# Attention and experts layer on one core: a block's weighted sums issued behind the next block's shift

## The chip, the cores and the metric

The kernel runs on one core of a Trainium2 chip. The metric is device time in microseconds (us) of the whole kernel, the median of several executions. Lower is better.

## The reference

The input is 16 batches of 512 tokens by 128 features, float32. Each batch goes through layernorm, an attention step and an expert step, each added back to its input:

```
qkv = layernorm(x) @ qkv_w.T                  # 16 heads of 8 features
c = mean of q per block . mean of k per block # 8 blocks of 64 tokens
mask: a block of queries sees its own block of keys and its one best block
x = x + softmax(q k / sqrt(8), masked) @ v @ proj_w.T + proj_b
logits = layernorm(x) @ wr + br               # 4 experts, the best 2 are kept
y_e = gelu(layernorm(x) @ w1_e + b1_e) @ w2_e + b2_e
x = x + sum over the kept experts of gate_e * (y_e, corrected by a constant)
```

## The kernel before, in words

Every engine has its own program, written out in order by hand (functions `tensor`, `vector`, `scalar`, `pool`, `sync`); the engines meet only at semaphores. TensorE, VectorE and ScalarE each run a loop over the batches b (0 to 15) and in it over the 8 blocks m of 64 queries. The work is software-pipelined over batches: while batch b has its attention, the second products of the experts of batch b - 2 are computed (`c_down`), the projections q, k, v of batch b + 1 (`project`), and behind the blocks the first products of the experts of batch b - 1 (`c_up`). Full overlap begins at b = 2.

TensorE's steps for one block m, b at least 2, in the order of lines 469 to 506:

- `weighted(b, m-1)` (L349, 32 matmuls): values times probabilities of the block before, into o_ps. It waits for the exponentials and for the copy of the values.
- `row_max(b, m)` (L329, two transposes): turns the maxima over the keys, which VectorE found (`block_max`, L657), into v_ps. It waits until v_ps is free.
- `scores(b, m+1)` (L310, 4 matmuls), into the other half of s_ps.
- `shift(b, m)` (L338, 16 matmuls): subtracts the row maxima from the scores in PSUM. It waits for VectorE's `row_max` (L666), which makes nmax from what TensorE's `row_max` turned.
- `o_rows` (L356, four transposes, blocks 2, 4, 6): a pair of blocks of weighted sums is turned back, after ScalarE has copied it (`o_copy`, L932). `o_columns` (L363, blocks 3, 5, 7) and `o_project` (L368, blocks 4, 6) follow for the pair.
- In blocks 2, 3, 4 `project` q, k, v of the next batch (L264 to L266); in block 5 the products of the block means (L293), from which VectorE selects the best key block (`a_select`, L637 to L648, ending in the index for a gather by DMA on POOL, L1030). In block 1 `a_columns` (L273) turns the next batch's normalised rows.
- `c_down` chunks 2m and 2m+1 (L406, two matmuls each). Four chunks make one expert's output in the bank y_ps, so a bank is complete with the last chunk of blocks 1, 3, 5 and 7.
- `values(b, m+1)` (L322): turns the next block's values into v_ps; ScalarE copies them to vaug (L917), which frees v_ps.

After block 7 follow `weighted(b, 7)`, the projection of pair 2 and 16 `c_up` steps; behind the 13th of them `begin(b + 1)` issues the next batch's first scores, which wait for the gathered keys (DMA keys<-kv_chosen).

VectorE's order in a block (L808 to L853): `row_max(b, m)` (L666), `block_max(b, m+1)` (L657), `o_project`, `o_rows` (reciprocal L673, product L676), then work of the other batches: in block 1 `a_columns` (L597), in block 2 sums and parts of q (L601, L606, L607), in block 3 the low part of k and the product of sums (L612, L613, L630), in block 5 the selection, in block 6 the ranking and split (L711 to L723, L702); last in odd blocks `c_gated(b - 2, m // 2)` (L753), which reads the completed bank y_ps.

ScalarE's order in a block (L970 to L989): in blocks 2, 4, 6 `o_copy` (L932), then `shift_exp` (L924, the exponentials), then copies of the projections (L897, L910, L905), `o_columns` (L939) and `values` (L917).

The lines that tie VectorE's two steps to TensorE's:

```
pe.wait_ge(bank_v.free, bank_v.at["max", b, m])       # L334, shift waits for VectorE's row_max
v.wait_ge(bank_v.full, bank_v.at["max", b, m])        # L663, VectorE's row_max waits for TensorE's
v.wait_ge(of.full, of.at["down", b, e])               # L745, c_gated waits for the fourth chunk
act.wait_ge(weighted_done, 2 * n + 2)                 # L929, o_copy waits for both blocks' sums
```

Of the kernel before, what the change touches and what calls it, by code (L numbers as in the profile page):

```python
# [21 lines left out]
M = N // BS  # L22
# [41 lines left out]
def layer(nc, x, wqkv_t, wproj_t, proj_b, w1, b1_t, w2, b2, wr, br, ident, head_sum,  # L64
          head_one, block_rank, row_mine, row_base, expert_before, expert_rows, own_block, head_mask,
          query_rows, key_rows, out):
    with ExitStack() as ctx:
# [172 lines left out]
        def stages(b):  # L240


            return (2, 0, 1, 3) if b == 0 else (2, 3, 4, 5)
# [18 lines left out]
        def tensor(pe):  # L262
# [13 lines left out]
            def a_columns(b):  # L276
                pe.wait_ge(xn_done, b + 1)
                columns(b, "xnT", xn)
# [188 lines left out]
            for b in range(B):  # L467
                ahead = b >= 1 and b + 1 < B
                for m in range(M):
                    if m >= 1 and b >= 2:  # L470
                        weighted(b, m - 1)
                    row_max(b, m)
                    if m >= 1 and b < 2:
                        weighted(b, m - 1)
                    edge = m in (0, M - 1)
                    if b >= 2 and edge:
                        c_down(b - 2, 2 * m)
                    if m + 1 < M:
                        scores(b, m + 1)
                    shift(b, m)  # L480
                    if b == 0 and m >= 3 or b == 1 and m not in (2, 3, 4):
                        keep_busy(5)
                    if b >= 1 and m == 0:
                        c_columns(b - 1)
                    if b >= 1 and m == 1:
                        c_route(b - 1, (2, 3))
                    if m in (2, 4, 6):
                        o_rows(b, (m - 2) // 2)
                    if m in (3, 5, 7):
                        o_columns(b, (m - 3) // 2)  # L490
                    if m in (4, 6):
                        o_project(b, (m - 4) // 2)
                    if ahead and m in stages(b)[:3]:
                        project(b + 1, "qkv"[stages(b).index(m)])
                    if ahead and m == stages(b)[3]:
                        a_products(b + 1)
                    if b >= 2 and not edge:
                        c_down(b - 2, 2 * m)
                    if ahead and m == 1:
                        a_columns(b + 1)  # L500
                    if b >= 2:
                        c_down(b - 2, 2 * m + 1)
                    if m + 1 < M:
                        values(b, m + 1)
                    if b >= 1 and m == 0:
                        c_route(b - 1, (0, 1))
                    if b == 0:
                        if m in stages(b)[:3]:
                            project(b + 1, "qkv"[stages(b).index(m)])
                        if m == stages(b)[3]:  # L510
                            a_products(b + 1)
                        if m >= 5:
                            (bias_out, bias_sum, bias_columns)[m - 5]()
# [17 lines left out]
            b = B - 1  # L531
# [31 lines left out]
        def vector(v):  # L563
# [242 lines left out]
            for b in range(B):  # L806
                ahead = b >= 1 and b + 1 < B
                for m in range(M):  # L808
# [19 lines left out]
                        block_max(b, m + 1)  # L828
                    if m in (4, 6):
                        o_project(b, (m - 4) // 2)  # L830
                    if m in (2, 4, 6):
                        o_rows(b, (m - 2) // 2)
                    if ahead and m == 0:
                        a_rows(b + 1)
# [14 lines left out]
                        c_gates(b - 1, ranked)  # L849
                    if b >= 2 and m % 2:  # L850
                        c_gated(b - 2, m // 2)
                    if b == 0 and m == 2:
                        bias_masked()  # L853
                o_project(b, T - 2)
# [16 lines left out]
            b = B - 1  # L871
# [20 lines left out]
        def scalar(act):  # L892
# [75 lines left out]
            values(0, 0)  # L968
            for b in range(B):
                for m in range(M):  # L970
                    if m in (2, 4, 6):
                        o_copy(b, (m - 2) // 2)
                    shift_exp(b, m)
                    if b >= 1 and m == 0:
                        c_columns(b - 1)
                    if b >= 1 and b + 1 < B and m == 1:
# [590 lines left out]
```

## Time and profile before

| | |
|---|---|
| median of 3 executions | 893.54 us (892.5 to 895.87) |
| the profiled execution: its time, its span | 900.17 us, 898.5 us |
| TensorE matmul busy, weight loads busy | 827.9 us (92%), 558.8 us (62%) |
| VectorE busy, ScalarE busy | 517.5 us (58%), 460.9 us (51%) |
| TensorE's granted clock, mean | 0.962 of full speed |

Busy times are sums of instruction durations. Matmuls are pipelined and their ends are modelled, so the distance from one group's start to the next group's start says more of TensorE's pace than its busy share. In the rows, PE is TensorE's matmul queue, PEld its weight loads, DVE VectorE, ACT ScalarE, POOL GpSimd. Idle time in square brackets is what the engine sat idle just before the group, and who released it.

### The profile page before, as it was taken

What the parts mean: (1) busy time and instruction counts of PE and PEld (TensorE: products, weight loads), DVE (VectorE), ACT (ScalarE), POOL (GpSimd) and SP (SyncE); (2) the same over time, 40 slices, a digit from 0 to 9 for tenths busy, and PEclk for the clock granted to TensorE, in tenths of its full rate; (3) what the DMA queues carried; (4) which work ended last, traced back from release to release, by engine and by line L of the source; (5) the groups of instructions that cost most, each with busy time, mean ns of one, the idle gap of its engine ahead of it and who ended that gap; (6) DMA issues with size and microseconds to landing.
All of it is one profiled execution on the core that took longest, in us unless ns stands there. A gap on an engine that the chain in (4) does not pass through costs nothing.

```text
span 898.5 us, 23529 instructions
## 1 busy us (share of the span) xinstructions
PE 827.9 (92%) x9382; PEld 558.8 (62%) x9382; DVE 517.5 (58%) x1526; ACT 460.9 (51%) x754; POOL 174.8 (19%) x176
## 2 busy tenths in 40 slices
PE   3287889999999999999999999999999999999995
PEld 2165667666666666676666567676666666666662
DVE  6073465746575665747566565757566666646321
ACT  2042247374655556374746457374646556473740
POOL 5300011210313031221213021221213031211111
PEclk8598599999999999999999999999999999999998
DMA  8987078676958668685957578675848676771110
GB/s 257 231 213 172 5 215 182 165 178 185 214 155 210 167 184 195 187 193 164 212 159 193 151 199 194 191 191 158 213 145 215 164 204 160 210 159 35 60 59 13
DMA packets 207440, 151.77 MB, mean 169 GB/s; under 512 B 123208, under 2 KB 189648, under 8 KB 203232
## 3 DMA queue, kind: packets, MB, share of 16 engines
q1 hardware_dynamic: 205024, 133.46, 59.8%
q0 software_dynamic: 2304, 16.78, 5.0%
q8 instruction: 76, 1.25, 0.6%
q14 instruction: 36, 0.29, 0.1%
HBM read 95.02 MB, written 50.99 MB: 163 GB/s over the span
## 4 chain that ended last, share of the span: by engine, by line
PE 61%; DMA 20%; ACT 8%; issue 5%; DVE 3%; SPq 2%; POOL 0%; POOLq 0%; ACTq 0%; DVEq 0%
PE y_ps L406 15%; DMA selected<-kv_table,index 8%; PE o_ps L349 6%; PE s_ps L310 5%; DMA kv_chosen<-selected 4%; PE s_ps L338 4%; PE s_ps L264 4%; ACT hid L960 4%; PE s_ps L266 4%; PE s_ps L265 4%; DMA kv_table<-stage 3%; PE o_ps L356 3%; PE a_ps L379 2%; PE v_ps L329 2%; DMA keys<-kv_chosen 2%
## 5 line engine op out<-in xcount | busy, mean ns | idle before, releaser
L406 PE MATMUL y_ps<-hid,w2s 128*128 128x512 f32 x480 | 236.1, 602 | 0.0
L657 DVE TRANSPOSE_TENSOR_REDUCE rmax<-s_ps 128x16 bf16<-128x512 f32 x256 | 168.2, 699 | 70.5 <-PE s_ps L310 70.4
L924 ACT ACTIVATE prob<-s_ps 128x1024 f32<-128x1024 f32 x128 | 131.1, 1024 | 150.6 <-PE s_ps L338 150.5
L960 ACT ACTIVATE hid<-s_ps,b1s 128x512 f32<-128x512 f32 x256 | 171.2, 688 | 38.8 <-PE s_ps L266 35.2
L1050 POOL TENSOR_TENSOR yT<-yT,gate_cols 128x512 f32<-128x512 f32 x48 | 61.4, 1279 | 294.7 <-DVE gate_cols L753 294.2
L310 PE MATMUL s_ps<-qdiag,keys 128*128 128x256 f32 x512 | 95.3, 309 | 24.8 <-DMA keys<-kv_chosen 24.7
L264 PE MATMUL s_ps<-xnhi,w1hi 128*128 128x512 f32 x256 | 113.1, 442 | 1.4
L406 PEld LDWEIGHTS y_ps<-hid,w2s 128*128 128x128 f32 x480 | 83.2, 193 | 43.8 <-issue 40.0
L917 ACT COPY vaug<-v_ps 128x128 f32<-128x128 f32 x128 | 33.9, 265 | 147.4 <-PE v_ps L322 147.3
L666 DVE TENSOR_REDUCE nmax<-v_ps 128x64 bf16<-128x256 bf16 x128 | 54.2, 423 | 95.4 <-PE v_ps L329 95.4
L266 PE MATMUL s_ps<-xnhi,w1lo 128*128 128x512 f32 x256 | 101.4, 396 | 0.0
L265 PE MATMUL s_ps<-xnlo,w1hi 128*128 128x512 f32 x256 | 100.9, 394 | 0.0
L349 PEld LDWEIGHTS o_ps<-prob,vaug 128*32 128x32 f32 x4096 | 64.1, 111 | 54.9 <-issue 41.8
L310 PEld LDWEIGHTS s_ps<-qdiag,keys 128*128 128x128 f32 x512 | 71.0, 195 | 39.0 <-issue 30.3
L349 PE MATMUL o_ps<-prob,vaug 128*32 128x64 f32 x4096 | 85.0, 224 | 0.0
L338 PEld LDWEIGHTS s_ps<-nmax,hone 64*128 64x128 bf16 x2048 | 37.7, 96 | 36.6 <-DVE nmax L666 32.7
L264 PEld LDWEIGHTS s_ps<-xnhi,w1hi 128*128 128x128 f32 x256 | 48.4, 189 | 19.1 <-ACT hid L960 8.8
L338 PE MATMUL s_ps<-nmax,hone 64*128 64x64 bf16 x2048 | 53.0, 193 | 4.9 <-DVE nmax L666 3.7
L266 PEld LDWEIGHTS s_ps<-xnhi,w1lo 128*128 128x128 f32 x256 | 48.1, 188 | 11.6
L932 ACT COPY oT<-o_ps 128x512 f32<-128x512 f32 x64 | 37.5, 587 | 32.5 <-PE o_ps L349 32.5
L265 PEld LDWEIGHTS s_ps<-xnlo,w1hi 128*128 128x128 f32 x256 | 48.7, 190 | 6.4 <-issue 0.7
L1030 POOL DMA_INDIRECT selected<-kv_table,index x16 | 17.7, 1104 | 157.6 <-DVE index L648 151.0
(143 smaller groups left out, 1051.5 us busy)
## 6 DMA issues: line engine op xcount, KB each, us to landing
qdiag<-q_table SPq DMA_DIRECT2D x128, 128.0 KB, 3.9
kv_chosen<-selected SPq DMA_DIRECT2D x32, 512.0 KB, 5.5
keys<-kv_chosen SPq DMA_DIRECT2D x32, 512.0 KB, 5.4
gate_cols<-gates SPq DMA_DIRECT2D x64, 256.0 KB, 4.2
kv_table<-stage SPq DMA_DIRECT2D x16, 768.0 KB, 3.9
q_table<-qpair SPq DMA_DIRECT2D x16, 512.0 KB, 3.0
xs<-in_x SPq DMA_DIRECT2D x16, 256.0 KB, 5.7
kv_table<-stage SPq DMA_DIRECT2D x16, 256.0 KB, 2.9
```

What stands on the lines that cost most here:

```text
L264: pe.matmul(dst, left_hi, right_hi, start=True, stop=False)
L265: pe.matmul(dst, left_hi, right_lo, start=False, stop=False)
L266: return pe.matmul(dst, left_lo, right_hi, start=False, stop=True)
L310: ins = pe.matmul(s_ps[i][:, g * HQ * BS:(g + 1) * HQ * BS].rearrange("p (h s) -> p h s", s=BS), keys[j][:, m, g, :], queries, start=g % 2 ...
L338: ins = pe.matmul(s_ps[i][:, half * N + h * BS:half * N + (h + 1) * BS], hone[r, h, :], nmax[i][r, :], start=False, stop=True, skip_group_ ...
L349: ins = pe.matmul(o_ps[32 * (h % HQ):32 * (h % HQ) + VW, h // HQ, i * BS:(i + 1) * BS], vaug[i][:, h, :], prob[i][:, h, :], start=True, st ...
L406: ins = pe.matmul(dst[:], w2s[:, n, :], hid[:, n, :], start=(c == 0), stop=(c == C - 1))
L657: v.tensor_reduce(rmax[m % 2][:, :, half * P // 2:half * P // 2 + HH].rearrange("p k h -> p h k"), s_ps[m % 2][:, half * N:(half + 1) * N] ...
L666: v.tensor_reduce(nmax[m % 2][:].rearrange("h (b c) -> h b c", b=2), v_ps[:, 0:P].bitcast(BF16).rearrange("h (b g c) -> h b c g", b=2, g=4 ...
L924: act.activation(prob[m % 2][:].rearrange("p h s -> p (h s)"), s_ps[m % 2][:], ACT.Exp, scale=SCALE).then_inc(exped, 1)
L960: act.activation(hid[:, k, :], up_ps[up_bank(k)], ACT.Gelu, bias=b1s[:, k:k + 1]).then_inc(gelued, 1)
L1050: g.tensor_tensor(yT[:], yT[:], gate_cols[(E * b + e) % NG][:], ALU.add).then_inc(summed, 1)
```

## The change

For b of at least 2, TensorE issues `weighted(b, m-1)` behind `shift(b, m)` instead of ahead of `row_max(b, m)`. `values(b, m+1)` and, in blocks 2, 4, 6, `o_rows` now stand ahead of the last chunk of `c_down` (2m+1); `o_rows` stood right behind `shift` before. VectorE takes its `o_rows` at the end of the block, behind `c_gated`, and ScalarE its `o_copy` behind `shift_exp`. For b = 0 and 1 all stays in place but that `values` moves in the text past lines that do nothing there. No instruction is added or removed.

```diff
@@ tensor
                 for m in range(M):
-                    if m >= 1 and b >= 2:
-                        weighted(b, m - 1)
                     row_max(b, m)
                     if m >= 1 and b < 2:
                         weighted(b, m - 1)
...
                     shift(b, m)
+                    if m >= 1 and b >= 2:
+                        weighted(b, m - 1)
...
-                    if m in (2, 4, 6):
+                    if m in (2, 4, 6) and b < 2:
                         o_rows(b, (m - 2) // 2)
...
                     if ahead and m == 1:
                         a_columns(b + 1)
+                    if m + 1 < M:
+                        values(b, m + 1)
+                    if m in (2, 4, 6) and b >= 2:
+                        o_rows(b, (m - 2) // 2)
                     if b >= 2:
                         c_down(b - 2, 2 * m + 1)
-                    if m + 1 < M:
-                        values(b, m + 1)
@@ vector
-                    if m in (2, 4, 6):
+                    if m in (2, 4, 6) and b < 2:
                         o_rows(b, (m - 2) // 2)
...
                     if b >= 2 and m % 2:
                         c_gated(b - 2, m // 2)
+                    if m in (2, 4, 6) and b >= 2:
+                        o_rows(b, (m - 2) // 2)
@@ scalar
-                    if m in (2, 4, 6):
+                    if m in (2, 4, 6) and b < 2:
                         o_copy(b, (m - 2) // 2)
                     shift_exp(b, m)
+                    if m in (2, 4, 6) and b >= 2:
+                        o_copy(b, (m - 2) // 2)
```

## Rows read from the trace of the kernel before

**Rows 1.** The page, part 1: busy time and share of the span by engine.

```profile
PE 827.9 (92%) x9382; PEld 558.8 (62%) x9382; DVE 517.5 (58%) x1526; ACT 460.9 (51%) x754; POOL 174.8 (19%) x176
```

**Rows 2.** The timeline of PE, two batches' same step (start us, us, engine, line, operation).

```profile
440.80 0.60 PE L422 MATMUL y_ps<-idn,yT 128*128 128x128 f32 x4
...
490.30 0.60 PE L422 MATMUL y_ps<-idn,yT 128*128 128x128 f32 x4
```

**Rows 3.** The timeline of PE and PEld at the head of block 3.

```profile
411.50 0.65 PE L349 MATMUL o_ps<-prob,vaug 128*32 128x64 f32 x32
...
412.08 0.28 PE L329 MATMUL v_ps<-idn,rmax 128*128 128x128 bf16 x2
412.15 0.54 PEld L310 LDWEIGHTS s_ps<-qdiag,keys 128*128 128x128 f32 x4
...
412.89 0.29 PEld L338 LDWEIGHTS s_ps<-nmax,hone 64*128 64x128 bf16 x16 [0.20 <-DVE nmax L666]
...
413.23 0.33 PE L363 MATMUL v_ps<-idn,att 128*128 128x128 f32 x1
```

**Rows 4.** The waits by engine: us in total, times, longest us.

```profile
PEld s_ps L338 <- DVE nmax L666: 32.7, 101, 3.1
...
PE s_ps L310 <- DMA keys<-kv_chosen: 24.7, 6, 16.9
...
PEld o_ps L349 <- ACT prob L924: 11.6, 14, 0.8
```

**Rows 5.** The timeline of PE and DVE, end of block 1 and head of block 2.

```profile
405.50 1.02 PE L406 MATMUL y_ps<-hid,w2s 128*128 128x512 f32 x2
...
406.32 0.69 DVE L597 TENSOR_TENSOR xnlo<-a_ps,xnhi 128x512 fp32r<-128x512 f32 x1 [0.61 <-ACT xnhi L897]
406.36 0.27 PE L322 MATMUL v_ps<-idn,vals 128*128 128x128 f32 x1
...
406.93 0.74 DVE L753 SCALAR_TENSOR_TENSOR yT<-y_ps,mT,gate_cols 128x512 f32<-128x512 f32 x1
407.15 0.29 PE L329 MATMUL v_ps<-idn,rmax 128*128 128x128 bf16 x2
...
407.59 0.41 DVE L666 TENSOR_REDUCE nmax<-v_ps 128x64 bf16<-128x256 bf16 x1
...
408.06 0.41 PE L338 MATMUL s_ps<-nmax,hone 64*128 64x64 bf16 x16
```

**Rows 6.** The timeline of ACT and DVE, end of block 3 and head of block 4.

```profile
414.29 0.58 ACT L910 CAST stage<-a_ps 128x512 fp32r<-128x512 f32 x1
...
416.11 0.22 DVE L630 TENSOR_TENSOR qk<-qsum,ksum 128x64 f32<-128x64 f32 x1
...
416.25 0.75 DVE L753 SCALAR_TENSOR_TENSOR gate_cols<-y_ps,mT,gate_cols 128x512 f32<-128x512 f32 x1
...
416.92 0.42 DVE L666 TENSOR_REDUCE nmax<-v_ps 128x64 bf16<-128x256 bf16 x1
```

**Rows 7.** The timeline of PE and DVE, end of block 5 and head of block 6.

```profile
423.14 1.94 PE L406 MATMUL y_ps<-hid,w2s 128*128 128x512 f32 x4
...
425.12 0.75 DVE L753 SCALAR_TENSOR_TENSOR gate_cols<-y_ps,mT,gate_cols 128x512 f32<-128x512 f32 x1
...
426.03 0.42 DVE L666 TENSOR_REDUCE nmax<-v_ps 128x64 bf16<-128x256 bf16 x1 [0.16 <-PE v_ps L329]
```

**Rows 8.** The timeline of PE and PEld, end of block 7.

```profile
431.71 1.02 PE L406 MATMUL y_ps<-hid,w2s 128*128 128x512 f32 x2
...
432.73 0.49 PEld L349 LDWEIGHTS o_ps<-prob,vaug 128*32 128x32 f32 x32 [0.83 <-ACT prob L924]
```

**Rows 9.** The timeline of PE: the longest wait for gathered keys after the start.

```profile
496.77 0.71 PE L310 MATMUL s_ps<-qdiag,keys 128*128 128x256 f32 x4 [2.03 <-DMA keys<-kv_chosen]
```

**Rows 10.** Windows: us, busy of PE, PEld, DVE, ACT, POOL, granted clock, DMA.

```profile
345.80:348.00 2.20, 2.10 (x11) 1.64 (x11) 1.32 (x2) 0.63 (x2) 0.00 (x0) 1.00 1.12 252
...
499.50:502.00 2.50, 2.50 (x8) 1.36 (x8) 0.42 (x1) 1.97 (x2) 0.00 (x0) 0.55 0.70 146
```

**Rows 11.** The timeline of PE: the wait for keys ahead of the first window above.

```profile
345.84 0.71 PE L310 MATMUL s_ps<-qdiag,keys 128*128 128x256 f32 x4 [1.30 <-DMA keys<-kv_chosen]
```

## The prediction, made before the changed kernel was run

> **What bounds the kernel now.** I read the page first, then the timeline of one steady batch, then the waits. By the page TensorE is busy nearly throughout and no other engine is busy for more than 58% of the span [rows 1]. The timeline says what a batch costs: the same step of two neighbouring batches starts 49.5 us apart [rows 2]. Within that stretch the matmul groups follow each other almost without a gap, so the batch is the sum of TensorE's steps, which run in program order, and of the short waits between them. A reordering that adds and removes nothing can therefore change only the waits.
>
> Which waits are there? Block 3 is typical [rows 3]. weighted takes 0.58 us from start to start (411.50 to 412.08). row_max starts at 412.08, the weights of the scores are loaded from 412.15 to 412.69, and shift's first weights only at 412.89: 0.20 us of waiting for nmax. From row_max to shift it is thus 0.81 us, and shift takes 0.34 us to the next step (413.23). This wait returns in nearly every block: 32.7 us of weight-load idling in 101 cases, some of it under running matmuls [rows 4]. What makes it is the round trip row_max on TensorE, nmax on VectorE, shift on TensorE. VectorE's nmax starts 0.32 to 0.33 us behind row_max's start when VectorE is free (412.08 to 412.41 in block 3, of which the row in block 6 shows the same: it follows row_max with 0.16 us of idling before it [rows 7]), takes 0.42 us, and shift starts 0.06 us after its end.
>
> The second thing to see is how nearly VectorE is late. In block 2 it comes from the low part of the normalised rows (406.32 to 407.01), goes at once into c_gated (406.93) and from that at once into nmax (407.59), which is 0.44 us behind row_max instead of 0.33 [rows 5]. Shift starts at 408.06, 0.91 us behind row_max. In block 4 c_gated (416.25 to 417.00) runs into nmax (416.92) with nothing between, on top of the chain of k: high part on ScalarE, sums and low part on VectorE, qk [rows 6]. In block 6 only 0.16 us is spare [rows 7]. In other words the time that VectorE needs for c_gated behind the last chunk of an odd block is hidden today by two of TensorE's steps: values and weighted, together 0.79 us (406.36 to 407.15 [rows 5]), 0.21 and 0.58.
>
> **The change, part by part.**
>
> *weighted behind shift, values ahead of the last chunk.* This takes both covers away. TensorE now goes from the last chunk straight to row_max, while c_gated cannot start before the last chunk has ended. And nothing is put between row_max and shift, so the 0.20 us stay. I follow the batch of the rows.
>
> Block 1: the weighted sums of block 0 move behind its shift, everything after them keeps its time; a_columns of the next batch and the chunk behind it too.
>
> Block 2: values takes the place at 405.50, the last chunk starts at 405.71 and row_max at 406.57 (a chunk takes 0.86 us, 405.50 to 406.36 [rows 5]), 0.58 us earlier than before. VectorE is no earlier: the low part still ends at 407.01; the bank is complete at 405.71 + 1.02 = 406.73, so c_gated starts at 406.93, nmax at 407.59, shift at 408.06, all as before. But weighted is then still to be done: **+0.58 us**.
>
> Block 3: VectorE's o_rows, some 0.5 us in two operations, now comes last in block 2, behind the parts of q. By my reckoning it ends about when nmax of block 3 is wanted. Bounds: 0 (it fits) and 0.10. I take **+0.04 us**.
>
> Block 4: the projection of k stands behind weighted, so it is 0.62 us later, and the whole chain of rows 6 with it, since it has no slack: shift comes 0.62 us later than before, with weighted of block 3 still to do: another **+0.58 us**.
>
> Block 5: block 4 is even, it has no c_gated; o_rows (two operations, about 0.5 us) ends before row_max's result is there. 0.
>
> Block 6: if the last chunk of block 5 starts at X, it ends at X + 1.02, c_gated starts at X + 1.06 (it started 0.04 us behind the end of the chunks, 425.08, in rows 7), nmax 0.67 us later as in rows 5 and 6 at X + 1.73, and shift at X + 1.73 + 0.42 + 0.06 = X + 2.21. Unhindered it would be X + 0.86 + 0.81 = X + 1.67. **+0.54 us**.
>
> Block 7: a chunk stands between row_max and shift and hides VectorE's ranking, split and o_rows; 0. Behind it weighted(b, 7) waited for its exponentials: it started at 432.73, the chunk before it at 431.71, a chunk is 0.86, so 0.16 us were lost [rows 8], in 14 batches [rows 4]. With weighted(b, 6) now in between this goes: **-0.16 us**.
>
> *exponentials ahead of the pair's copy; o_rows late.* ScalarE's exponentials come up to 0.6 us earlier in blocks 2, 4, 6, but nobody waits for them there. The copy starts about 1.0 us behind shift and o_rows is asked for some 2.4 us behind it, under weighted, projection and chunk; that cover is enough, so 0. Without it the copy (0.6 us) would show. The copy of values (0.27 us) must be done before row_max; its cover is the last chunk, 0.86 us, so 0. The result goes on to o_columns a block later, unaffected. On SP and POOL nothing is moved.
>
> *The gathered keys.* Four times after the start the next batch's first scores wait for keys, 1.0 to 2.0 us (24.7 us in 6 cases with 16.9 at the start [rows 4]; the longest is in rows 9). The gather hangs on the selection in block 5, which is delayed by 0.58 + 0.04 + 0.58 = 1.20 us, while the scores are delayed by 1.58; these waits shrink by 0.38 us each: **-1.5 us** over the kernel.
>
> **Sum.** 0.58 + 0.04 + 0.58 + 0.54 - 0.16 = 1.58 us a batch by the rows; I take 1.5, as small successions (transposes before a chunk rather than before other short steps) may give back some hundredths. The order changes for b = 2 to 15, 14 batches: +21.0, less 1.5: +19.5 us. The profiled execution had 900.17 us (span 898.5), so 919.7 there. That is 6.63 us above the median of 893.54, much of it the waits for keys; against the median it makes **913.0 us**.
>
> **Rivals.**
>
> 1. *VectorE is late only in block 2* (the others have some slack that starts do not show): 14 x (0.58 - 0.16) = +5.9, 899.4 us; with one more block 907. For it: only block 2 shows a late nmax already. Against: rows 6 and 7 have 0 and 0.16 us of slack, and 0.79 us of cover go. Chance 0.08.
>
> 2. *The clock falls as well.* After a wait of 2.03 us for keys [rows 9] the granted clock of a stretch of 2.5 us was 0.55, about the lower of its levels, 1.2 GHz [rows 10]; that cost 2.5 x 0.45 = 1.1 us. After a wait of 1.30 us [rows 11] it was full, 2.4 GHz [rows 10]. The new waits are about 0.7 us, three times a batch. If they brought such a fall once a batch, that adds 14 x 1.1 = 15.4: 928 us. [...] Chance 0.04.
>
> 3. *No change.* VectorE gets c_gated done in time after all (the bank is complete earlier than the modelled ends say), and only the 0.16 us are gained: 14 x 0.16 = 2.2, 891.3 us. Chance 0.08.
>
> 4. *Faster.* The wait of shift for nmax vanishes, because row_max starts earlier in the block. By rows 3 it is 0.20 us of loading; in 7 blocks of 14 batches 98 x 0.20 = 19.6, plus 2.2: 872 us. It decides where nmax ends before the scores' weights are in, 0.61 us behind row_max's start; nmax's own round trip is 0.33 + 0.42 + 0.06 = 0.81. That speaks against it, as nothing enters between the two. The Trainium skill (Trainium Kernel Development and Optimization, "Best Practices") would have the distance to the limit judged by the weight loads' busy share, not the matmuls'; by that, 62% leaves room for such a gain, but the timeline shows TensorE's matmul groups following each other without gaps, whatever the share of the loads. Chance 0.04.
>
> **How the numbers follow.** The forecast has 0.76. A measurement of this kernel can tell about 0.5% (4.5 us) from no change. Slower by more than that: forecast, rivals 1 and 2, 0.88; same 0.08; faster 0.04. The range reaches from rival 1 with a second block late (some way below 907) to the forecast with all terms at their upper ends (1.7 a batch, nothing given back at the keys: 917) and a few falls of the clock: 903 to 922.
>
> **What would show it.** Batches 51 us apart in the steady part instead of 49.5. In blocks 2, 4, 6 the weight load of shift idles 0.7 to 0.9 us for nmax, in 3, 5 still 0.2; c_gated starts right behind the last chunk or the low part, and nmax right behind c_gated, 1.0 us behind row_max instead of 0.33. weighted(b, 7) no longer waits for exponentials. The waits for keys are a little shorter. I am wrong if nmax in block 2 starts earlier than 0.9 us behind row_max, or if the copy of values or o_rows shows up as what TensorE waits for.

## The result, and the profile after

The changed kernel takes **903.12 us** (median of 7 executions, 900.37 to 904.16). The kernel before takes 892.5 us on the same chip (7 executions, 890.39 to 899.19). The ratio is 1.0106, 95% interval 1.0078 to 1.0133: 10.6 us slower, where 19.5 had been forecast. The profiled execution after has 900.37 us and a span of 898.7 us, which is 0.2 us more than the span before; why that is not the change's cost is worked out below.

The page, part 1, of the kernel after:

```profile
PE 811.9 (90%) x9382; PEld 550.7 (61%) x9382; DVE 520.3 (58%) x1526; ACT 455.9 (51%) x754; POOL 175.1 (19%) x176
```

TensorE is busy for less time than before (827.9 us in [rows 1]) in an equal span: the time is in waits. The waits by engine after (us in total, times, longest us):

```profile
PEld s_ps L338 <- DVE nmax L668: 56.6, 101, 3.6
...
PE s_ps L338 <- DVE nmax L668: 28.4, 45, 3.4
...
PE s_ps L310 <- DMA keys<-kv_chosen: 17.7, 2, 17.3
PEld v_ps L322 <- ACT attT L943: 17.4, 32, 1.3
...
PEld o_ps L349 <- ACT prob L928: 10.8, 15, 0.8
```

Beside [rows 4] this says two things. Shift's wait for VectorE has grown from 32.7 to 56.6 us, and now the matmuls wait as well as the weight loads, 45 times (28.4 us; before, 3 times and 3.7 us). The scores' wait for the gathered keys has gone from 24.7 us in 6 cases to 17.7 in 2, of which 17.3 are the start. One change made TensorE wait more and less.

The head of block 2 after, in the timeline of all engines, answers to [rows 5]:

```profile
400.00 1.02 PE L406 MATMUL y_ps<-hid,w2s 128*128 128x512 f32 x2
...
400.71 0.69 DVE L599 TENSOR_TENSOR xnlo<-a_ps,xnhi 128x512 fp32r<-128x512 f32 x1 [0.62 <-ACT xnhi L901]
...
400.99 0.27 PE L329 MATMUL v_ps<-idn,rmax 128*128 128x128 bf16 x2
...
401.32 0.74 DVE L755 SCALAR_TENSOR_TENSOR yT<-y_ps,mT,gate_cols 128x512 f32<-128x512 f32 x1
401.98 0.41 DVE L668 TENSOR_REDUCE nmax<-v_ps 128x64 bf16<-128x256 bf16 x1
...
402.44 0.41 PE L338 MATMUL s_ps<-nmax,hone 64*128 64x64 bf16 x16 [0.65 <-DVE nmax L668]
...
402.78 0.65 PE L349 MATMUL o_ps<-prob,vaug 128*32 128x64 f32 x32
```

row_max starts at 400.99. VectorE is still at the low part (to 401.40), takes c_gated, and reaches nmax 0.99 us behind row_max, where it took 0.44 before; shift's matmuls wait 0.65 us. Weighted comes behind them and covers nothing. The starts of shift in the eight blocks of this batch, from TensorE's timeline after:

```profile
393.72 0.41 PE L338 MATMUL s_ps<-nmax,hone 64*128 64x64 bf16 x16
...
397.12 0.41 PE L338 MATMUL s_ps<-nmax,hone 64*128 64x64 bf16 x16
...
402.44 0.41 PE L338 MATMUL s_ps<-nmax,hone 64*128 64x64 bf16 x16 [0.65 <-DVE nmax L668]
...
407.26 0.41 PE L338 MATMUL s_ps<-nmax,hone 64*128 64x64 bf16 x16
...
412.42 0.41 PE L338 MATMUL s_ps<-nmax,hone 64*128 64x64 bf16 x16 [0.54 <-DVE nmax L668]
...
417.43 0.41 PE L338 MATMUL s_ps<-nmax,hone 64*128 64x64 bf16 x16
...
421.91 0.41 PE L338 MATMUL s_ps<-nmax,hone 64*128 64x64 bf16 x16 [0.54 <-DVE nmax L668]
...
426.54 0.41 PE L338 MATMUL s_ps<-nmax,hone 64*128 64x64 bf16 x16
```

From shift to shift both kernels do the same work (one weighted lies between them in either order; only in the first stretch there is none after, so 0.58 us are added to its 3.40, and the last stretch, to weighted(b, 7), has one too many, so 0.58 is taken off):

| stretch | before, us | after, us | difference |
|---|---|---|---|
| block 0 to 1 | 4.07 | 3.98 | -0.09 |
| 1 to 2 | 4.74 | 5.32 | +0.58 |
| 2 to 3 | 4.83 | 4.82 | -0.01 |
| 3 to 4 | 4.51 | 5.16 | +0.65 |
| 4 to 5 | 5.07 | 5.01 | -0.06 |
| 5 to 6 | 4.04 | 4.48 | +0.44 |
| 6 to 7 | 4.70 | 4.63 | -0.07 |
| 7 to weighted(b, 7) | 1.52 | 1.46 | -0.06 |

The sum is +1.38 us. The steady batch has gone from 49.5 us [rows 2] to 50.87 (the step of [rows 2] starts at 385.79 and 436.66), that is +1.37.

**Where the time went.** The same step lies in every batch, the first time at the end of b = 2. Its first start fell at 189.46 us before and 182.15 after; over the profiled executions of all kernels here this start varied between 182 and 194 us, and the code up to b = 1 is the same, so these 7.3 us are not put down to the change. The clock has a part in them: in the first 190 us the mean granted clock was 0.85 of full speed before and 0.91 after. The twelve batches that follow took 603.59 us before and 610.97 after. Before, 12 x 49.5 make 594.0, and the other 9.6 lie in every third batch (51.61, 51.2, 53.4 and 51.26 us long), those that wait for keys. Not all of the 9.6 is waiting for keys: the four waits of the first scores are 5.9 us (1.51, 1.30, 2.03 and 1.03), some more is waiting for the gathered values just behind them, and in the batch of 53.4 us about 1.5 us is the clock. After the wait of 2.03 us it fell to its lower level. The windows of before and of after have

```profile
498.00:502.00 4.00, 4.00 (x13) 2.27 (x12) 1.03 (x3) 2.78 (x4) 0.00 (x0) 0.57 0.86 184
```

```profile
190.00:840.00 650.00, 623.96 (x7487) 420.15 (x7486) 403.44 (x1174) 358.74 (x598) 124.27 (x122) 1.00 0.67 173
```

where the third number from the end is the granted clock: about half before in those 4 us, in which the batch's lag behind its neighbours grew from 2.4 us (at 497.52) to 3.9 (at 504.29), and full after in all twelve batches.

After, 12 x 50.87 make 610.4, and 0.5 is left. So the twelve batches lost 12 x 1.37 = 16.4 us in the order of the steps and got back 9.1 at the keys: +7.4 net. With b = 2 as well that is about 8.8, and the executions say 10.6, between 7.0 and 11.9 by the interval. In b = 15 next to nothing was lost (47.61 against 47.72 us).

**Why the waits for keys are gone.** Each batch writes its keys to a table in DRAM (768 KB), the values behind it, and then, once the write has landed, reads its own keys from it (SP's queue). The page, part 3, has a queue of instruction packets (packets, MB, share of the same 16 DMA engines):

```profile
q8 instruction: 76, 1.25, 0.6%
```

They are 16 KB each. I take them to be the fetches of TensorE's program: nothing names them so, but filler matmuls, which change TensorE's program alone, move them (see e13 and e14). The timeline of SP before, in a batch whose successor's scores waited 2.03 us [rows 9]:

```profile
469.52 0.38 SPq L1111 DMA_DIRECT2D kv_table<-stage  x1
469.94 2.26 SPq L1115 DMA_DIRECT2D vals<-stage  x1
...
474.54 0.73 SPq L1121 DMA_DIRECT2D keys<-kv_table  x1
```

and the DMA queues before in the stretch 469 to 470 us (packets, MB, share of 16 engines):

```profile
q8 instruction: 1, 0.02, 6.4%
```

One instruction packet, 6.4% of sixteen engines over 1 us, so one engine for about 1 us. It starts some 0.5 us behind the write's issue, and the keys are read 5.0 us behind it. After the change, in the batch that answers to it:

```profile
466.09 0.38 SPq L1117 DMA_DIRECT2D kv_table<-stage  x1
466.52 0.67 SPq L1121 DMA_DIRECT2D vals<-stage  x1
470.06 0.73 SPq L1127 DMA_DIRECT2D keys<-kv_table  x1
```

Here the keys are read 3.97 us behind. Over the whole kernel before, a packet fell 0.5 to 0.8 us behind the write in exactly every third batch (writes at 168.67, 319.29, 469.52, 621.92 and 772.26 us); there the keys were read 4.6 to 5.2 us behind the write, in all others 4.0. In the profile after, packets fall at about -2.5, -1.0 and +4.9 us from the write, and it is 4.0 to 4.1 always.

From the late write to TensorE's wait the way is long. Behind the four writes that a wait followed, the gather's instruction on POOL starts up to 0.4 us later than elsewhere, the gathered rows land 15.5 to 16.6 us behind the write (14.2 to 14.7 in the steady batches between), and the first of the gathered keys 26.0 to 27.0 us behind it (23.2 to 23.8). The first scores ask for them 25.2 us behind it. Why the delay of about 1 us has grown to some 3 by then is not shown. All this is so far two traces side by side; the second half of the experiments is about it.

### The profile page after: what moved, and what is told of

It reads as the page before. It is cut to its first block, busy times and chain, and to the rows that moved or that the text cites. A ratio compares the mean times of both kernels' runs of the same rounds, so it can differ in the third digit from the quotient of the medians.

```text
span 898.7 us, 23529 instructions
## 1 busy us (share of the span) xinstructions
PE 811.9 (90%) x9382; PEld 550.7 (61%) x9382; DVE 520.3 (58%) x1526; ACT 455.9 (51%) x754; POOL 175.1 (19%) x176
## 4 chain that ended last, share of the span: by engine, by line
PE 69%; DMA 10%; ACT 8%; issue 6%; DVE 4%; SPq 2%; POOL 0%; DVEq 0%; POOLq 0%; ACTq 0%
PE y_ps L406 19%; PE o_ps L349 7%; PE s_ps L264 5%; PE s_ps L338 5%; PE s_ps L266 4%; PE s_ps L265 4%; ACT hid L964 4%; DMA selected<-kv_table,index 4%; PE s_ps L310 4%; PE o_ps L356 3%; DMA kv_chosen<-selected 3%; PE v_ps L368 2%; PE a_ps L379 2%; DVE nmax L668 2%; ACT L928 2%
## 5 line engine op out<-in xcount | busy, mean ns | idle before, releaser
L406 PE MATMUL y_ps<-hid,w2s 128*128 128x512 f32 x480 | 245.5, 600 | 0.0
L310 PE MATMUL s_ps<-qdiag,keys 128*128 128x256 f32 x512 | 93.2, 305 | 17.7 <-DMA keys<-kv_chosen 17.7
L406 PEld LDWEIGHTS y_ps<-hid,w2s 128*128 128x128 f32 x480 | 78.3, 194 | 14.2 <-issue 10.0
L338 PE MATMUL s_ps<-nmax,hone 64*128 64x64 bf16 x2048 | 52.6, 192 | 28.7 <-DVE nmax L668 28.4
L338 PEld LDWEIGHTS s_ps<-nmax,hone 64*128 64x128 bf16 x2048 | 37.3, 95 | 60.3 <-DVE nmax L668 56.6
L349 PEld LDWEIGHTS o_ps<-prob,vaug 128*32 128x32 f32 x4096 | 63.1, 110 | 17.3 <-ACT prob L928 10.8
L329 PEld LDWEIGHTS v_ps<-idn,rmax 128*128 128x128 bf16 x256 | 22.1, 102 | 63.7 <-issue 58.1
```

The source lines that it names most:

```text
L310: ins = pe.matmul(s_ps[i][:, g * HQ * BS:(g + 1) * HQ * BS].rearrange("p (h s) -> p h s", s=BS), keys[j][:, m, g, :], queries, start=g % 2 ...
L338: ins = pe.matmul(s_ps[i][:, half * N + h * BS:half * N + (h + 1) * BS], hone[r, h, :], nmax[i][r, :], start=False, stop=True, skip_group_ ...
L349: ins = pe.matmul(o_ps[32 * (h % HQ):32 * (h % HQ) + VW, h // HQ, i * BS:(i + 1) * BS], vaug[i][:, h, :], prob[i][:, h, :], start=True, st ...
L406: ins = pe.matmul(dst[:], w2s[:, n, :], hid[:, n, :], start=(c == 0), stop=(c == C - 1))
```

## The experiments

Three questions: is the loss VectorE's c_gated in front of nmax; is the gain the fetches beside the table write; and, what came up on the way, why some executions of the kernel before are longer than others. The expectations name some theories by letter; the fetch in the table write stands against the new order by itself (later scores, other neighbours on the queues) as what took the waits away. Runs that stand together in a paragraph with one number for the kernel before ran on the same chip.

### Is it VectorE's order?

**e4**: the kernel after, and on VectorE `c_gated` behind the next block's `row_max`. TensorE keeps the new order.

```diff
                     row_max(b, m)
+                    if b >= 2 and m in (2, 4, 6):
+                        c_gated(b - 2, m // 2 - 1)
...
-                    if b >= 2 and m % 2:
+                    if b >= 2 and m == M - 1:
                         c_gated(b - 2, m // 2)
```

> The changed kernel, with VectorE's c_gated of blocks 1, 3 and 5 taken behind row_max of the next block (2, 4, 6) instead of ahead of it. Theory A (VectorE comes late to nmax because c_gated starts only behind the last chunk, which row_max now follows at once): nmax starts 0.33 us behind row_max in blocks 2, 4 and 6, the batch falls from 50.87 to 49.3 us and the time to 880 to 884 us. Rival (the lateness comes from the copies or from o_rows that moved): blocks 2, 4 and 6 keep 0.5 us or more of waiting and the time stays within 4 us of 903.

Measured: 884.57 us against 900.1 of the kernel before, ratio 0.9822 [0.9748, 0.9895]; batches of 49.33 us. The timeline of all engines in e4, head of block 2:

```profile
449.55 0.69 DVE L599 TENSOR_TENSOR xnlo<-a_ps,xnhi 128x512 fp32r<-128x512 f32 x1 [0.62 <-ACT xnhi L903]
...
449.83 0.27 PE L329 MATMUL v_ps<-idn,rmax 128*128 128x128 bf16 x2
...
450.16 0.42 DVE L668 TENSOR_REDUCE nmax<-v_ps 128x64 bf16<-128x256 bf16 x1
450.49 0.74 DVE L755 SCALAR_TENSOR_TENSOR yT<-y_ps,mT,gate_cols 128x512 f32<-128x512 f32 x1
450.63 0.29 PEld L338 LDWEIGHTS s_ps<-nmax,hone 64*128 64x128 bf16 x16 [0.20 <-DVE nmax L668]
```

nmax is back at 0.33 us behind row_max and c_gated follows it. e4's waits show what is left of shift's:

```profile
PEld s_ps L338 <- DVE nmax L668: 31.9, 101, 3.1
```

56.6 us have become 31.9, the value of before [rows 4]. Everything else of the change is in e4, so the whole loss per steady batch (50.87 - 49.33 = 1.54 us) is c_gated in front of nmax, and the rest of the change gives 49.5 [rows 2] - 49.33 = 0.17 us a batch. Some of e4's batches are longer (up to 50.42 us), in part because `values` waits for the gathered values.

**e10**: the kernel after, with `values` behind the last chunk again, so that row_max's wait for v_ps stands without cover.

```diff
-                    if m + 1 < M:
-                        values(b, m + 1)
                     if m in (2, 4, 6) and b >= 2:
                         o_rows(b, (m - 2) // 2)
                     if b >= 2:
                         c_down(b - 2, 2 * m + 1)
+                    if m + 1 < M:
+                        values(b, m + 1)
```

> The changed kernel, but with values(b, m+1) behind the last chunk again, so that row_max follows values at once. Theory A (row_max must wait for ScalarE's copy of values, 0.31 + 0.27 + 0.06 = 0.64 us behind its start, where weighted hid it before): row_max comes 0.43 us later behind values than their 0.21 us in blocks 3 to 7; in blocks 4 and 6 this takes the place of most of the wait for c_gated. Batches of 51.5 to 52.5 us, 912 to 926 us. Rival (only c_gated delays, the copy is hidden): 50.7 to 50.9 us as in the changed kernel, 905 us.

Measured: 933.46 us in one execution (before: 894.85); batches of 52.63 us. Both are somewhat above what was expected, 912 to 926 and 51.5 to 52.5. The waits of e10:

```profile
PE v_ps L329 <- ACT vaug L921: 42.1, 93, 0.8
```

row_max now waits for ScalarE's copy of the values, 0.45 us each time in steady blocks, where after the change this wait is 4.2 us in 8 cases, all told. Once weighted no longer stands between values and row_max, values has to go ahead of a chunk: the two moves of the change belong together.

### Is shift's 0.20 us for nmax a loss? (rival 4)

**e6**: e4 with weighted between row_max and scores, so that shift is asked for 0.58 us later and nmax is ready.

```diff
-                    if m >= 1 and b < 2:
+                    if m >= 1:
                         weighted(b, m - 1)
...
                     shift(b, m)
-                    if m >= 1 and b >= 2:
-                        weighted(b, m - 1)
```

> The changed kernel with c_gated of blocks 1, 3, 5 behind the next row_max and with weighted(b, m-1) between row_max and scores instead of behind shift. Theory A (the 0.2 us that shift waits for nmax are a round trip which weighted covers, once neither c_gated nor the copy of values delays row_max): from row_max to shift 1.22 us with the weighted sums in it, instead of 0.80 plus 0.58; 0.16 us less in each of blocks 1 to 6, batches of 48.4 us instead of 49.33, 870 to 874 us. Rival (the keys become the bound, since the gather is asked for earlier by less than the scores): waits for keys of 0.5 to 1 us in most batches, 880 us.

Measured: 908.46 us against 901.09, ratio 1.0091 [1.0061, 1.0121]; batches of 51.02 us. That is at least 34 us more than expected. TensorE's timeline in e6:

```profile
477.50 0.27 PE L329 MATMUL v_ps<-idn,rmax 128*128 128x128 bf16 x2
477.71 0.65 PE L349 MATMUL o_ps<-prob,vaug 128*32 128x64 f32 x32
478.29 0.73 PE L310 MATMUL s_ps<-qdiag,keys 128*128 128x256 f32 x4
478.96 0.41 PE L338 MATMUL s_ps<-nmax,hone 64*128 64x64 bf16 x16
```

From scores to shift it is 0.67 us although nmax has long been there, against 0.71 in [rows 3] (412.18 to 412.89). The "0.20 <- nmax" before shift's weight load was nearly all hidden under the scores' own matmuls: 0.04 us of it was loss. And row_max to weighted takes 0.21 us rather than 0.10 to the scores, so that row_max to shift with weighted in it takes 1.46 us in the plain blocks, more than the 0.79 + 0.58 of the kernel after. Weighted right behind row_max also waits for what is made late: in block 3 row_max to shift took 1.84 us, in block 7 mostly 2.07. Rival 4's 19.6 us were not there to be had.

### Are the waits for keys the fetches in the table write?

The idea: if the fetches come at fixed places of TensorE's program, adding or removing filler matmuls at the start (`keep_busy`, two instructions per unit) moves them against the writes. Only that number is edited:

```diff
-            keep_busy(16)
+            keep_busy(20)
```

20 in e2, 40 in e7, 48 in e13, 52 in e14 for the kernel before; 12 in e3 and 34 in e8 for the kernel after.

**e1, e2, e3** (before: 900.1 us). The kernel before once more, and both with a little filler more or less:

> The kernel before once more, for a second profile of it. Theory A (the cause is in the program): TensorE's batches are again 49.5 us apart but for every third one, which is 1.7 to 3.9 us longer because the first scores of the next batch wait for the gathered keys, and in just these batches the 16 KB instruction packet on queue q8 starts 0.5 to 0.8 us behind the issue of the table write (kv_table<-stage, 768 KB), so that the keys of the own block are issued 4.6 to 5.2 us behind it instead of 4.0. Theory B (chance of the profiled execution): the waits stand in other batches or are gone, and the time is nearer to 885 us.

> The kernel before with 4 more idle matmuls (8 instructions with their weight loads) in TensorE's warm-up at the start, where it waits for data anyway; all code after it lies 8 instructions further on. Theory A (the keys come late where an instruction fetch of TensorE falls into the table write): the fetch in every third batch moves from +0.6 us to about -1.0 us relative to the write's issue, the write takes 4.0 us everywhere, the waits for keys go, 882 to 886 us. Theory B (the waits come from the period of the transfers or from chance): nothing changes, 892 us with waits of 1 to 2 us in every third batch.

> The changed kernel with 4 fewer idle matmuls in the warm-up. Theory A: the fetches that stand 1.0 us ahead of the table write in every third batch move to about +0.6 us, the write takes 4.6 to 5.2 us there, and the waits for keys come back in every third batch, smaller than before (0.5 to 1.5 us): 905 to 909 us against 903 of the changed kernel. Theory B (the later scores of the changed order hide the keys whatever the fetches do): 903 us, no waits.

e1: 901.82 us; fetches 0.5 to 1.7 us behind the write in every third batch and own keys read 4.9 to 5.5 us behind it, much as in the first trace, so the pattern belongs to the program. Once more it came in a batch that is not a third one (write at 723.57 us): there the fetch was at +0.6 and the keys at 5.15, where the first trace has the fetch at -0.5 and 3.95 in the same batch. e2: 900.04 us, ratio 0.9993 [0.9956, 1.003], fetches at +0.6 to +1.0, late writes as before (4.4 to 5.2). e3: 905.16 us, ratio 1.0051 [1.0012, 1.0091], fetches at about -2, -0.1 to -1.2 and +4.9, all writes 4.0 to 4.1, no waits for keys in the steady batches. Eight instructions hardly move a fetch, so e2 and e3 decide nothing. e3 has batches of 50.87 us as the kernel after. But e1 had batches of 50.35 us, not 49.5; on that see below.

**e7, e8** (before: 901.09 us).

> The kernel before with 24 more idle matmuls (48 instructions) in the warm-up. The 8 instructions of the first try hardly moved the fetches. Theory A (fetches in the table write make it late): the fetch of every third batch leaves the range 0 to 3.5 us behind the write's issue for about -1 us, and the own keys are issued 4.0 us behind the write in all batches; if another batch's fetch enters the range instead, that batch has the late write. Theory B (what is late is that batch, not the fetch): the write stays late by 0.6 to 1.2 us in the same batches 2, 5, 8, 11, 14 wherever the fetch stands.

> The changed kernel with 18 more idle matmuls (36 instructions) in the warm-up. Theory A: in every third batch a fetch enters the range 0 to 3.5 us behind the table write's issue, the own keys are issued 4.5 to 5.2 us behind it there instead of 4.0, and a wait for keys of up to 1 us shows. Theory B: the write takes 4.0 us everywhere as in the changed kernel, whose batches are 50.87 us.

e7: 902.94 us; the fetch of the third batches stayed at +0.5 to +1.3 and their keys at 5.1 to 5.2 behind the write. Other fetches moved to +5.4, without effect. No decision. e8: 909.88 us; the fetch at +4.9 moved to +3.8 to +4.0, the end of the write. The timeline of SP in e8:

```profile
470.32 0.38 SPq L1117 DMA_DIRECT2D kv_table<-stage  x1
470.75 0.66 SPq L1121 DMA_DIRECT2D vals<-stage  x1
476.25 0.73 SPq L1127 DMA_DIRECT2D keys<-kv_table  x1
```

5.93 us instead of 3.97. In the five batches with such a fetch it was 4.58, 4.45, 5.93, 5.94 and 4.54, in all others 3.96 to 4.06. Behind the two of 5.9 waits for what is gathered were back in the new order of steps, 0.84 us for values and 1.21 us for keys, in batches of 52.79 and 52.43 us. So the order by itself doesn't take them away: the fetch theory holds, the other falls. (e8 is one execution, and its 909.88 us are not compared.)

**e13, e14** (before: 892.74 us), the test from the other side: the kernel before, with the fetches moved out.

> The kernel before with 32 more idle matmuls (64 instructions) in the warm-up. In e2 and e7 (8 and 48 instructions) the fetch of every third batch stayed 0.6 us behind the table write's issue. Theory A (the fetch makes the write late, the late write the waits for keys): with 64 instructions it leaves the write, the own keys are issued 4.0 us behind the write in those batches, the waits for keys go, and the median is 5 to 9 us below the kernel before on the same chip (less where block 6 waits for nmax and hides them). Theory B (it is the batch, not the fetch): the write stays late by 0.6 to 1.2 us in batches 2, 5, 8, 11, 14, ratio 1.0.

> The same with 36 more idle matmuls (72 instructions), in case 64 are not enough. Theory A: as for 64 instructions; whichever batches have a fetch between 0 and 4 us behind the write's issue, these and only these have the own keys issued later than 4.1 us behind it. Theory B: as there.

e13: 892.14 us, ratio 0.9976 [0.9942, 1.001]. The packet came at +0.4 to +0.5 in four of the five third batches (keys read 5.0 to 5.2 us behind the write) and at -0.6 in one, at 315.70 us; there it was 3.96, and its batch 49.5 us. e14: 890.8 us, ratio 0.9967 [0.9943, 0.9992], the packets at -0.5 to -0.9 in all five. The timeline of SP in e14:

```profile
461.93 0.38 SPq L1111 DMA_DIRECT2D kv_table<-stage  x1
462.35 0.67 SPq L1115 DMA_DIRECT2D vals<-stage  x1
...
465.89 0.73 SPq L1121 DMA_DIRECT2D keys<-kv_table  x1
```

its DMA queues from 461 to 462 us, and its waits:

```profile
q8 instruction: 1, 0.02, 7.0%
```

```profile
PE s_ps L310 <- DMA keys<-kv_chosen: 11.8, 3, 9.1
```

The packet is there, but ahead of the write. 3.96 us; all but one of the writes have 3.96 to 4.04 (one 4.38, with a fetch at +3.6). Eleven of the twelve batches are 49.5 to 49.6 us. The other, the first, has 50.56: it waits 0.65 us for gathered values and has the late write of 4.38. Of the three waits for keys that are left none lies in the twelve. So the kernel before has lost them in its old order, by 36 more units of filler (72 instructions) at its start. The profiled execution has a span of 886.1 us.

Over all 16 traces there are 224 such writes from b = 2 on. Behind the 36 with a fetch 0.4 to 1.7 us after their issue the own keys were read 4.40 to 5.68 us after it, behind the 9 with one at 3.6 to 4.0 us 4.05 to 5.94, behind the 9 at 4.2 to 4.4 us 4.02 to 4.42, and behind the other 170 3.95 to 4.13, with one exception of 4.33. No fetch fell between 1.7 and 3.6 us. This settles for the profiled executions what made the writes late and the waits come.

The medians don't confirm the size. e14 is 0.3% faster, 1.9 us, where 5 to 9 had been expected, and e13 0.2%, not told from nothing. The filler itself costs nothing that the trace shows: it ends at 32.8 us, and the first scores wait for keys until 41.91 (42.18 before). Nor is it the clock: straight lines through time against mean granted clock put e14's executions only 1.6 us below those of the kernel before at 0.972. The other executions were not profiled, so why they gain so little stays open. The median of the kernel after speaks for a gain at the keys of about 7 us: 13 x 1.37 = 17.8 were lost by the order and 10.6 measured.

### What else: block 6 in some sessions

In e1 the kernel before had 0.85 us more in block 6 of nine of the twelve batches. All engines of e1 there:

```profile
477.02 1.10 POOL L1030 DMA_INDIRECT selected<-kv_table,index  x1 [7.25 <-DVE index L648]
...
477.12 0.29 PE L329 MATMUL v_ps<-idn,rmax 128*128 128x128 bf16 x2
...
478.40 0.59 ACT L932 COPY oT<-o_ps 128x512 f32<-128x512 f32 x1 [1.49 <-PE o_ps L349]
478.44 0.42 DVE L666 TENSOR_REDUCE nmax<-v_ps 128x64 bf16<-128x256 bf16 x1 [1.15 <-PE v_ps L329]
...
478.92 0.41 PE L338 MATMUL s_ps<-nmax,hone 64*128 64x64 bf16 x16 [0.99 <-DVE nmax L666]
```

c_gated had long ended (477.29); row_max's result was there; yet VectorE's nmax and ScalarE's copy both start only at 478.4, some 0.3 us behind the end of POOL's gather instruction. In the first session, and in those of e9 to e12 and e13 and e14, nmax starts 0.32 us behind row_max in this block; in the sessions of e1 to e4 and e5 to e8 it was 1.17 to 1.36 in most batches of the old order. That fits with the 900.1 and 901.09 us that the kernel before has there and the 892.5 to 894.85 in the others (nine times 0.85 make 7.7 us). It is not a matter of the chip alone: e5 to e8 and e13 and e14 ran on the same one.

In these sessions it goes with the place of POOL's instruction. Of the 36 batches of e1, e2 and e7 it starts 0.09 to 0.26 us ahead of row_max in 26, and there nmax is 1.17 to 1.36 us behind row_max; in the other 10, where a late table write had pushed it to 0.07 to 0.47 us behind row_max, nmax is 0.32 to 0.74 us behind.

**e5**: the kernel after in such a session.

> The changed kernel, timed beside the kernel before on the chip of the coming runs. In the last runs the kernel before took 900 us on its chip instead of 892.5, its batches 50.35 us instead of 49.5, because in block 6 nmax started 1.17 us behind row_max instead of 0.32, where POOL's gather instruction stood. Theory A (the changed order keeps row_max of block 6 out of the gather instruction's way): 903 to 906 us here too, batches of 50.87 us, so that the loss against the kernel before is 1.1% on one chip and about 0.4% on another. Theory B (the chip slows both alike): 911 us, ratio 1.011.

905.06 us against 901.09, ratio 1.0043 [1.0011, 1.0074]; batches of 50.87 us, without the hold-up: in the new order the gather instruction starts 0.24 us *behind* row_max's start. So the change costs 1.1% in one kind of session and 0.4 to 0.5% in the other (e5 and e3), with the same 903 to 905 us of its own.

**e9, e11, e12** (before: 894.85 us). e9 is the kernel before with e4's edit on VectorE, e11 is e4 once more, and e12 lets POOL's gather wait for the matmuls of row_max in block 6:

```diff
+                if b >= 3:
+                    g.wait_ge(bank_v.full, bank_v.at["max", b - 1, 6])
```

> The kernel before, with c_gated of blocks 1, 3, 5 behind the next row_max as in e4, and nothing else. Theory A (in the old order values and weighted hide c_gated, so its place hardly matters): block 2 gains the 0.10 us that nmax was late there, batches 0.1 us shorter than those of the kernel before on the same chip, ratio 0.997 to 1.0. Rival (the gain of e4 is that of c_gated's place alone, whatever TensorE's order): about 885 us.

> The kernel of e4 once more, for a second interval. If its gain is real: batches of 49.3 to 49.6 us and 882 to 887 us, ratio 0.975 to 0.99. If it was the luck of one set of executions: within 5 us of the kernel before.

> The kernel before, with POOL's gather instruction waiting besides for TensorE's row_max of block 6, so that it starts about 0.3 us behind row_max's start instead of 0.27 us ahead of it. Theory A (where nmax of block 6 is 1.2 us behind row_max on this chip, the gather instruction, which starts between weighted and row_max, holds up what VectorE and ScalarE wait for): nmax follows row_max by 0.33 us again, batches of 49.5 us where the keys are there in time; the gather is 0.6 us later, so more batches wait for keys; 893 to 899 us. Theory B (the lateness has nothing to do with the gather's moment): nmax stays 1.2 us behind, batches 50.4 us and longer, 901 us or more.

e9: 894.91 us, ratio 0.9997 [0.996, 1.0033]; batches of 49.4 us, 0.1 shorter, but the keys waits stayed (27.6 us in 7 cases in its waits, every third batch): the edit on VectorE alone is worth nothing. e11: 883.17 us, ratio 0.9882 [0.982, 0.9944], steady batches of 49.12 us, five of the twelve longer (49.4 to 50.6): the version of both orders together beats both kernels in this kind of session too. e12: 895.88 us, ratio 1.0 [0.9966, 1.0034]. This chip had no hold-up to remove (batches of 49.5 us in either), so e12 tells nothing of it; it shows only that the gather, issued 1.34 us later, took 7.3 to 9.4 us rather than the 8.8 to 10.9 of the first trace, and the keys were hardly later. Whether POOL's instruction itself holds the two engines or something that goes with it, and why in two sessions only, stays open.

## Why the prediction was half right

- **The bound and the method**: right. TensorE is in order and gapless, and the change touched waits alone.
- **Block 2, +0.58**: measured +0.58 from shift to shift; nmax 0.99 us behind row_max, forecast 1.0.
- **Block 3, +0.04**: measured -0.01; nmax at 0.36 us instead of 0.33, so o_rows did just fit.
- **Block 4, +0.58**: +0.65. Of this 0.54 is nmax. The rest is, as I read it, an item that the prediction put at nothing ("The result goes on to o_columns a block later, unaffected"): o_columns now comes while values is asked for earlier, and values waits for ScalarE's copy of attT (17.4 us of weight-load idling in 32 cases; from the chunk's start at 409.04 to values at 410.05 it takes 1.01 us rather than the 0.86 of a chunk, 0.15 lost).
- **Block 6, +0.54**: nmax came exactly that late (shift 1.34 us behind row_max instead of 0.80), the stretch grew by 0.44.
- **Block 7, -0.16**: only -0.06. The exponentials are no longer late (they end at 428.01, weighted starts at 428.58), although the row still names them; but TensorE takes 0.95 us from the chunk to weighted all the same. A wait's name had long been done.
- **"Small successions may give back some hundredths"**: they gave back 0.06 to 0.09 in blocks 1, 5 and 7 each. Per batch +1.37 against 1.5 taken: a size, over 13 batches 1.7 us. And b = 15, counted as the 14th with 1.5 us, lost 0.11.
- **The 0.20 us of [rows 3]**: read as a loss in nearly every block. By e6 it was 0.04, the rest being hidden; the forecast kept it on both sides, so only rival 4 hung on it.
- **The gathered keys, -1.5 us**: this is the step that failed. "These waits shrink by 0.38 us each" took them as a transfer of fixed length against which the scores come a little later. Measured is -9.1 us in the twelve steady batches: the transfer's own length came from a 16 KB fetch of TensorE's program beside the table write, and moving TensorE's instructions against the rest of the kernel moved the fetch out of it (e8 brings it back in the new order, e14 takes it out in the old one). I had read the length of the wait [rows 9] and not what made it come in every third batch only. That the fetch moved out of the write, and not into it, is luck: the change was not made for it.
- **The base**: the profiled execution was taken as 6.63 us above the median, much of it for these waits, and the forecast then kept them. That reading isn't shown: profiled executions of other sessions have the waits too and lie within 4 us of their medians, and this one had more of the lower clock in its start (a mean of 0.85 over its first 190 us, 0.91 in the kernel after). With -9.1 in place of -1.5 and 1.37 in place of 1.5 over 13 batches the sum is about 8.8 instead of 19.5; 10.6 was measured.
- **The rivals**: 1 (late only in block 2) is refuted by the 0.54 and 0.44 us of blocks 4 and 6, though its time was near; 2 by the granted clock of the steady part after, 1.00, which the waits of 0.54 to 0.65 us, three a batch, did not bring down (the means over the whole span, 0.977 after and 0.962 before, differ by the start and say nothing of it). The Trainium skill (TensorE: Matmul & The Clock Gate, "Why this matters for your kernels") warns of idle gaps between bursts of matmuls, but of longer ones than these; for these the trace agrees. The fall behind the 2.03 us had cost about 1.5 us by the steps' starts, not the 1.1 of the prediction. 3 fell with the first batch, and 4 with e6.

## What to carry to other kernels

When a step is moved ahead on the engine that sets the pace, look at what its partner does in the freed cover: here one VectorE instruction of 0.74 us, in program order ahead of the one that TensorE waits for, cost more than the move gained, and swapping the two turned 1.1% slower into 1.2% faster (and 0.4 to 0.5% slower into 1.8% faster in the sessions where block 6 of the kernel before was held up). A wait that comes in every third round of a loop in which all rounds do the same may have a cause outside the loop's own dependences; look in the DMA queues for the fetches of the program, and compare a round that waits with one that doesn't. And before an "idle" of a weight load is counted as a loss, see whether the matmul groups around it start any closer where the wait is absent.

## What the runs showed of the hardware

- A 16 KB packet of the instruction queue takes one DMA engine for about 1 us (0.88 to 2.1). A 768 KB write, issued 0.4 to 1.7 us ahead of such a packet, released its reader 0.4 to 1.7 us late (4.4 to 5.7 instead of 4.0 us); with the packet at its end (+3.6 to +4.4) it was 0 to 1.9 us late. Packets 0.1 us ahead of the write and earlier did it no harm.
- Filler at the start of TensorE's program moved the packets of every third batch by 1.1 to 1.7 us against the write with 72 instructions, by 1.2 us in one batch of five with 64, and with 48 or 8 not by more than they differ between two executions of the kernel before.
- In two sessions of five, VectorE and ScalarE both started an instruction only some 0.3 us behind the end of POOL's gather instruction (1.10 us), 0.85 us late, where this instruction began ahead of row_max; in the other three, in the same program, neither did. Open.
- After a wait of 2.03 us TensorE's granted clock fell to about half (0.57 from 498 to 502 us, its lower level, 1.2 GHz); 36 waits of 0.54 to 0.65 us in twelve batches left it full (2.4 GHz).
- From the start of the scores' matmuls to the start of shift's it is 0.71 us with a row that says 0.20 us of waiting, and 0.67 us without any wait (e6).
